# Weighted values over 64 keys a product, and an outer butterfly mixed while its matrix is turned

## The chip, the cores and the metric

The kernel runs on one core of a Trainium2 chip. A core has a matrix engine (TensorE, PE in the profile; PEld is its weight load), VectorE (DVE), ScalarE (ACT), GpSimd (POOL), a queue engine (SyncE, SP) and 16 DMA engines. The metric is the device time of one execution in microseconds (us); less is better. All data are float32.

## What is computed

Four layers in a row on x of 32 x 256 x 128, each `x = x + layer(layernorm(x))`: window attention, a butterfly FFN, linear attention, and the same FFN again. What matters here:

```python
# window attention: 16 heads of 8, 2 key heads, windows of 32 queries over 64 keys
scores = jnp.einsum('bhntd,bhnud->bhntu', qb, kb)
win_mask = (u >= t) & (u < t + W)            # t in 0..31, u in 0..63
probs = jax.nn.softmax(jnp.where(win_mask, scores, -jnp.inf), axis=-1)
out = jnp.einsum('bhntu,bhnud->bhntd', probs, vb)
# FFN: h = x @ W_exp + b_exp; nine butterfly stages; gelu; nine more; @ W_con
# stage s pairs feature i with i ^ 2**s:  na = w00 * a + w01 * b;  nb = w10 * a + w11 * b
```

Of every window's 64 keys exactly 32 count for each query: key u if u >= t in the first half, key u if u - 32 < t in the second.

## The kernel before, in words

The 8192 rows are cut into 16 groups of 512 rows (4 tiles of 128, two batches). A group passes through stages named P (input, keys and queries), W (window attention), F (first FFN), L (linear attention) and G (second FFN). Each engine's program is one list of steps, run in turns: `due(t, lag)` runs a step for group t - lag, so steps of up to eight groups are in flight. The tables PRODUCTS, VECTOR, PHI, PROBS and so on repeat that order, and the counts that one engine waits for on another are worked out from them. So the order on every engine is written out by hand, and each queue runs strictly in order. TensorE's results go to four ring banks in PSUM, one pair of banks for scores (`ps_s`) and one for weighted values (`ps_o`). On SP's queue stand the loads of x, the keys' and values' round trip through DRAM (`store_keys`, `spread_keys` with 8 DMAs, `spread_values` with 8 DMAs) and the stores of the result. `kx` has one buffer: the keys of a group are spread only when all four score products of the group ahead are done.

Window attention for one tile j (a chunk; four chunks a group, 64 in all):

- `scores` (L491): 8 products into `ps_s`; a row of `ps_s` is a query, 64 score columns for each of 16 heads.
- VectorE: `merge_halves` (L1018) puts the second half's score over the first's where t < row, so that 32 of 64 columns remain per head; `row_max` (L1025), `subtract_max` (L1031), and `scores_transposed` (L1038) in blocks of 32 by 32.
- ScalarE: `probs_out` (L810) writes exp of 512 values a row to `probs_m`.
- GpSimd: `probs_parted` (L419) writes `probs_t`, twice as wide: the same 512 values times either of two 0/1 masks `keep`, one part for each half of the keys.
- TensorE: `weighted_values` (L508): 16 products of 32 keys each; those of the second half add to the first's in PSUM. A row of ones in the values gives the sum of probabilities.
- VectorE: `head_outputs` (L1045 to L1052) transposes, takes the reciprocal and scales.

The FFN's nine butterfly stages are folded once, at the start, into one matrix each way. For the up matrix, seven inner stages go through TensorE (`up_stage`, L626, steps X.u0a to X.u6b) and ScalarE (L861); two outer stages, which pair whole blocks of 128 features, ran on VectorE (`up_outer_stage` by `outer_stage`, L286 and L289); `up_transposed` (L648) turns the four blocks with a matrix transpose against the identity, and ScalarE copies them to `w1b`. The down matrix has its outer stages first, on VectorE (`down_outer_stage`, `d_t`), then L640.

```python
nc.tensor.matmul(ps_o[32 * c:32 * c + 32, a, 0:HPK * WIN], vx[rows, j, a, u],
                 probs_t[rows, j % 2, u, a], start=(u == 0), stop=(u == PARTS - 1))
```

Of the kernel before, what the change touches and what calls it, by code (L numbers as in the profile page):

```python
# [9 lines left out]
ALU = mybir.AluOpType  # L10
# [7 lines left out]
WIN = 32  # L18
# [11 lines left out]
PARTS = SPAN // WIN  # L30
STAGES = HID.bit_length() - 1
INNER = P.bit_length() - 1
KVW = DIM + HEADS
FIRST = [("ident", P), ("last_half", WIN), ("keep", PARTS * WIN), ("wq", P), ("wkv", 2 * KV * HD), ("bq", 1), ("bkv", 1), ("inside", TSPAN), ("bo", P)]
# [33 lines left out]
]  # L68
PHI = [
    ("L.k1", 5), ("L.q", 4), ("L.k0", 4),  # L70
]
PROBS = [
    ("W.E3", 3), ("W.E0", 2), ("W.E1", 2), ("W.E2", 2),
# [1227 lines left out]
```

## Time and profile before

| | before |
|---|---|
| median of 3 runs | 597.85 us (596.56 to 598.96) |
| profiled execution, its own time | 597.42 us |
| its span | 595.6 us |
| TensorE busy, products | 553.9 us, 93% (6068) |
| TensorE weight loads | 355.3 us, 60% |
| VectorE | 445.7 us, 75% |
| ScalarE | 336.7 us, 57%, of it 77.0 for 60 table loads |
| GpSimd | 446.7 us, 75%, of it 150.4 for 64 masks |
| mean DMA rate | 38 GB/s |

The span is the time from the first to the last event of the profiled execution; its own time is what the same metric as the runs' gives for it. The share of busy time is an average over the filling, the middle and the end. Matmuls are counted by pass: each float32 product shows as two.

### The profile page before, as it was taken

What the parts mean: (1) busy time and instruction counts of PE and PEld (TensorE: products, weight loads), DVE (VectorE), ACT (ScalarE), POOL (GpSimd) and SP (SyncE); (2) the same over time, 40 slices, a digit from 0 to 9 for tenths busy, and PEclk for the clock granted to TensorE, in tenths of its full rate; (3) what the DMA queues carried; (4) which work ended last, traced back from release to release, by engine and by line L of the source; (5) the groups of instructions that cost most, each with busy time, mean ns of one, the idle gap of its engine ahead of it and who ended that gap; (6) DMA issues with size and microseconds to landing.
All of it is one profiled execution on the core that took longest, in us unless ns stands there. A gap on an engine that the chain in (4) does not pass through costs nothing.

```text
span 595.6 us, 16572 instructions
## 1 busy us (share of the span) xinstructions
PE 553.9 (93%) x6068; PEld 355.3 (60%) x6068; DVE 445.7 (75%) x1270; ACT 336.7 (57%) x574; POOL 446.7 (75%) x645
## 2 busy tenths in 40 slices
PE   3867698989999999999999999999999999999986
PEld 2533354556756656666666675665666666777663
DVE  5498878898888878787887888787877878654430
ACT  1321355366667666665666566766666666766532
POOL 6064778798979878897979798887887795956530
PEclk9996989999999999999999999999999999999998
DMA  9410201010101020111101010101010100000001
GB/s 316 134 37 15 52 7 46 13 41 16 39 24 46 25 47 20 33 37 29 43 21 43 16 42 26 45 26 43 21 34 20 29 24 2 19 3 19 0 19 35
DMA packets 37904, 22.48 MB, mean 38 GB/s; under 512 B 8384, under 2 KB 35520, under 8 KB 37824
## 3 DMA queue, kind: packets, MB, share of 16 engines
q1 hardware_dynamic: 35376, 17.21, 11.1%
q10 hardware_dynamic: 2448, 4.22, 2.0%
q8 instruction: 48, 0.79, 0.6%
q14 instruction: 32, 0.26, 0.2%
HBM read 15.91 MB, written 5.51 MB: 36 GB/s over the span
## 4 chain that ended last, share of the span: by engine, by line
PE 82%; DVE 7%; issue 3%; POOL 2%; DMA 1%; ACTq 1%; SPq 1%; ACT 1%; DVEq 0%; POOLq 0%
PE ring L523 20%; PE ring L535 18%; PE ps_o L508 10%; PE ps_s L491 9%; PE ring L472 7%; PE ring L546 5%; PE ring L566 4%; PE ring L606 3%; PE ring L555 2%; PE ring L583 2%; PE ring L576 1%; DVE u_t L289 1%; SPq L328 1%; DMA x_P<-in_x 1%; PE ring L595 1%
## 5 line engine op out<-in xcount | busy, mean ns | idle before, releaser
L419 POOL TENSOR_TENSOR probs_t<-probs_m,first 128x1024 f32<-128x1024 f32 x64 | 150.4, 2362 | 34.7 <-ACT probs_m L810 26.3
L792 ACT ACT_TABLE_LOAD x60 | 77.0, 1283 | 10.8 <-issue 9.7
L802 ACT ACTIVATE hid_G<-ring,b 128x512 f32<-128x512 f32 x64 | 44.0, 687 | 62.0 <-PE ring L523 61.2
L491 PE MATMUL ps_s<-kx,q_t 64*32 64x512 f32 x1024 | 71.0, 611 | 6.8 <-DVE merged L1031 4.3
L508 PE MATMUL ps_o<-probs_t,vx 32*32 32x256 f32 x2048 | 72.5, 392 | 3.1 <-DVE vx L1113 2.8
L523 PE MATMUL ring<-xT_G,w1b 128*128 128x512 f32 x128 | 65.7, 619 | 1.7 <-DVE x_F L1003 1.0
L1018 DVE COPY_PREDICATED ps_s<-first,ps_s 128x512 f32<-128x512 uint32 x64 | 43.6, 682 | 28.0 <-PE ps_s L491 27.6
L535 PEld LDWEIGHTS ring<-w,hid_G 128*128 128x128 f32 x512 | 59.5, 192 | 3.5 <-ACT hid_G L802 1.7
L535 PE MATMUL ring<-w,hid_G 128*128 128x128 f32 x512 | 59.9, 275 | 1.8 <-DVE x_L L1003 1.0
L523 PE MATMUL ring<-xT_F,w1b 128*128 128x512 f32 x128 | 59.2, 605 | 0.7 <-ACT xT_F L780 0.7
L535 PE MATMUL ring<-w,hid_F 128*128 128x128 f32 x512 | 59.9, 275 | 0.0
L535 PEld LDWEIGHTS ring<-w,hid_F 128*128 128x128 f32 x512 | 58.6, 192 | 0.8 <-issue 0.8
L802 ACT ACTIVATE hid_F<-ring,b 128x512 f32<-128x512 f32 x64 | 43.9, 687 | 23.3 <-PE ring L523 23.2
L810 ACT ACTIVATE probs_m<-merged_t 128x512 f32<-128x512 f32 x64 | 39.4, 620 | 22.4 <-POOL probs_t L419 17.2
L1045 DVE STREAM_TRANSPOSE ps_o<-ps_o 128x512 f32<-128x512 f32 x64 | 45.5, 711 | 7.6 <-PE ps_o L508 7.3
L508 PEld LDWEIGHTS ps_o<-probs_t,vx 32*32 32x32 f32 x2048 | 31.5, 106 | 29.1 <-DVE mv_W L982 10.6
L1031 DVE TENSOR_TENSOR merged<-ps_s,rowmax 128x512 f32<-128x512 f32 x64 | 44.0, 687 | 2.8
L523 PEld LDWEIGHTS ring<-xT_F,w1b 128*128 128x128 f32 x128 | 23.0, 189 | 36.4 <-issue 34.5
L1038 DVE STREAM_TRANSPOSE merged_t<-merged 128x512 f32<-128x512 f32 x64 | 44.4, 695 | 0.2 <-ACT probs_m L810 0.2
L1025 DVE TENSOR_REDUCE rowmax<-ps_s 128x16 f32<-128x512 f32 x64 | 43.1, 674 | 0.9 <-issue 0.3
L523 PEld LDWEIGHTS ring<-xT_G,w1b 128*128 128x128 f32 x128 | 21.4, 194 | 22.3 <-issue 21.3
L566 PEld LDWEIGHTS ring<-later,xT_L 128*128 128x128 f32 x128 | 23.2, 189 | 14.7 <-issue 12.3
(114 smaller groups left out, 1071.5 us busy)
## 6 DMA issues: line engine op xcount, KB each, us to landing
kx<-kv_rows SPq DMA_DIRECT2D x128, 40.0 KB, 2.2
x_P<-in_x SPq DMA_DIRECT2D x16, 256.0 KB, 3.2
out_x<-x_G SPq DMA_DIRECT2D x16, 256.0 KB, 2.3
vx_t<-kv_rows SPq DMA_DIRECT2D x128, 8.0 KB
up_s<-in_up_m ACTq DMA_DIRECT2D x7, 256.0 KB, 7.0
down_s<-in_down_m ACTq DMA_DIRECT2D x7, 256.0 KB, 6.9
kv_rows<-kv_t SPq DMA_DIRECT2D x16, 80.0 KB, 1.6
later<-in_later_c SPq DMA_DIRECT2D x1, 584.0 KB, 4.1
```

The source lines that it names most:

```text
L419: nc.gpsimd.tensor_tensor(probs_t[:, j % 2].rearrange("p u k h t -> p u (k h) t"), probs_m[:, j % 2].rearrange("p (a k) h t -> p a (k h) t ...
L491: last = nc.tensor.matmul(ps_s[32 * i:32 * i + 32, a], q_t[half, P * j + 32 * c:P * j + 32 * c + 32], kx[half, :, TSPAN * j + 32 * c:TSPAN ...
L508: last = nc.tensor.matmul(ps_o[32 * c:32 * c + 32, a, 0:HPK * WIN], vx[rows, j, a, u], probs_t[rows, j % 2, u, a], start=(u == 0), stop=(u ...
L523: nc.tensor.matmul(bank(name)[:], w1b[:, P * c:P * (c + 1)], x_t[s][:], start=True, stop=True).then_inc(product.sem, 1)
L535: last = nc.tensor.matmul(bank(name)[:, P * j:P * (j + 1)], hid[s][:, c, P * j:P * (j + 1)], w2[:, c], start=(c == 0), stop=(c == CH - 1))
L566: last = nc.tensor.matmul(bank(name)[:, 2 * P * i:2 * P * (i + 1)], x_t["L"][:, P * j:P * (j + 1)], wl_s[:, P:3 * P], start=True, stop=True)
L792: nc.scalar.activation(unused[:, i:i + 1], half[0:1, 0:1], function)
L802: nc.scalar.activation(hid[s][:, c], bank(name)[:], ACT.Gelu, bias=b1[:, c:c + 1]).then_inc(drained[BANK[name]].sem, 1)
L1018: nc.vector.copy_predicated(merged_s, last_half.bitcast(mybir.dt.uint32).rearrange("p (a t) -> p a t", a=1) .to_broadcast([P, HEADS, WIN]) ...
L1031: nc.vector.tensor_tensor(merged[:, j % 2].rearrange("p k h t -> p (k h) t"), halves()[0], m, ALU.subtract).then_inc(drained["S"].sem, 1)
L1038: nc.vector.transpose(merged_t[:, j % 2].rearrange("p k h t -> p (k h t)"), merged[:, j % 2].rearrange("p k h t -> p (k h t)")).then_inc(v ...
L1045: nc.vector.transpose(ps_o[:, :, 0:HPK * WIN], ps_o[:, :, 0:HPK * WIN]).then_inc(vec.sem, 1)
```

## The change

**Weighted values.** The value rows are laid out so that 64 rows of the array hold both halves of a window's 64 keys (WINDOW, `spread_values`); a chunk is then 8 products of 64 rows by 32 columns, each complete in itself. Its moving operand needs the probabilities of one window on both halves of the 64 rows. `probs_out` therefore writes exp of the scores twice (1024 values a row, straight to `probs_t`, which now has four buffers, one for each chunk), and the new `spread_probs` on SP's queue overwrites, with 4 DMAs a chunk of 32 rows x 2 KB each, one copy on every block of 32 rows by its neighbour's. `probs_parted` then masks in place, with a mask chosen by the row. `probs_m` is gone.

**Butterfly.** `up_outer_stage` is gone. `up_diagonals` on GpSimd multiplies the coefficients of both outer stages into 16 numbers a row (`up_mix`) and those with the identity into 16 diagonal blocks (`up_diag`). `up_transposed` multiplies each of the four blocks with a row of four diagonal blocks and adds up in PSUM, so mixing and turning are one product. `up_bias_out` mixes the bias column on VectorE.

**Order.** All orders are new (lags are counted from another start, which by itself moves nothing; TURNS goes from NG + 7 to NG + 10 for that). The table rows are left out of the diff, and the lists of `turn` too.

```diff
@@
-FIRST = [("ident", P), ("last_half", WIN), ("keep", PARTS * WIN), ("wq", P), ...
+FIRST = [("ident", P), ("last_half", WIN), ("keep", WIN), ("wq", P), ...
-WINDOW = [[0, 1, 2, 3], [1, 0, 3, 2]]
+WINDOW = [[0, 1, 2, 3], [2, 3, 0, 1]]
-        vx = sb("vx", [P, TILES, KV, PARTS, 32])
+        vx = sb("vx", [P, TILES, KV, PAIR, 32])
-        probs_m = sb("probs_m", [P, 2, KV, HPK, WIN])
-        probs_t = sb("probs_t", [P, 2, PARTS, KV, HPK, WIN])
+        probs_t = sb("probs_t", [P, TILES, PAIR, KV, HPK, WIN])
@@ spread_values
-                        c = WINDOW[kv][i]
+                        c = WINDOW[kv][i & ~1] + i % PARTS
+            def spread_probs(g, j):
+                sp.wait_ge(probs.sem, probs.after(g, f"W.E{j}"))
+                for i in range(4):
+                    own, other = slice(32 * i, 32 * i + 32), slice(32 * (i ^ 1), 32 * (i ^ 1) + 32)
+                    sp.dma_start(probs_t[other, j, i % PAIR].rearrange("p k h t -> p (k h t)"),
+                                 probs_t[own, j, i % PAIR].rearrange("p k h t -> p (k h t)")
+                                 ).then_inc(spread[j].sem, 16)
+            def up_diagonals():
+                pool.wait_ge(outer_in, 16)
+                pool.wait_ge(first_in, 16)
+                for far in range(2):
...
+                    nc.gpsimd.tensor_tensor(
+                        up_mix[:, 2 * far:2 * far + 2].rearrange("p f (b o) -> p f b o", b=2), near.to_broadcast([P, 2, 2, 2]),
+                        outer_far.to_broadcast([P, 2, 2, 2]), ALU.mult).then_inc(up_mixed, 1)
+                pool.wait_ge(up_mixed, 2)
+                for c in range(CH):
+                    nc.gpsimd.tensor_tensor(
+                        up_diag[:, c], ident.rearrange("p (a n) -> p a n", a=1).to_broadcast([P, CH, P]),
+                        up_mix[:, c].rearrange("p (o a) -> p o a", a=1).to_broadcast([P, CH, P]), ALU.mult
+                    ).then_inc(up_diag_made, 1)
@@ probs_parted
-                pool.wait_ge(product.sem, product.after(g if j >= 2 else g - 1, f"W.PV{(j - 2) % 4}"))
-                pool.wait_ge(probs.sem, probs.after(g, f"W.E{j}"))
+                pool.wait_ge(spread[j].sem, spread[j].after(g, f"W.d{j}"))
+                parts = probs_t[:, j].rearrange("p s k h t -> p (s k h) t")
                 nc.gpsimd.tensor_tensor(
-                    probs_t[:, j % 2].rearrange("p u k h t -> p u (k h) t"),
-                    probs_m[:, j % 2].rearrange("p (a k) h t -> p a (k h) t", a=1).to_broadcast([P, PARTS, HEADS, WIN]),
-                    keep.rearrange("p (u a t) -> p u a t", u=PARTS, a=1).to_broadcast([P, PARTS, HEADS, WIN]), ALU.mult
+                    parts, parts, keep.rearrange("p (a t) -> p a t", a=1).to_broadcast([P, PAIR * HEADS, WIN]), ALU.mult
                 ).then_inc(parted.sem, 1)
@@ weighted_values
-                for u in range(PARTS):
+                for s in range(PAIR):
                     for a in range(KV):
-                        for i in range(4):
-                            rows, c = slice(32 * i, 32 * i + 32), WINDOW[a][i]
-                            last = nc.tensor.matmul(ps_o[32 * c:32 * c + 32, a, 0:HPK * WIN], vx[rows, j, a, u],
-                                                    probs_t[rows, j % 2, u, a], start=(u == 0), stop=(u == PARTS - 1))
+                        for b in range(2):
+                            rows, c = slice(64 * b, 64 * b + 64), WINDOW[a][2 * b + s]
+                            last = nc.tensor.matmul(ps_o[32 * c:32 * c + 32, a, 0:HPK * WIN], vx[rows, j, a, s],
+                                                    probs_t[rows, j, s, a], start=True, stop=True)
@@ up_transposed
-                pe.wait_ge(up_outer, 4 * CH)
+                pe.wait_ge(up_diag_made, CH)
                 for c in range(CH):
-                    last = nc.tensor.transpose(bank("X.wT")[:, P * c:P * (c + 1)], u_t[INNER % 2][:, c, 0:P],
-                                               ident[:])
+                    last = nc.tensor.matmul(bank("X.wT")[:], u_t[INNER % 2][:, c, 0:P],
+                                            up_diag[:, c].rearrange("p o n -> p (o n)"), start=(c == 0), stop=(c == CH - 1))
@@ probs_out
-                act.wait_ge(parted.sem, parted.after(g if j >= 2 else g - 1, f"W.um{(j - 2) % 4}"))
+                act.wait_ge(product.sem, product.after(g - 1, f"W.PV{j}"))
                 act.wait_ge(vec.sem, vec.after(g, f"W.tr{j}"))
-                nc.scalar.activation(probs_m[:, j % 2].rearrange("p k h t -> p (k h t)"),
-                                     merged_t[:, j % 2].rearrange("p k h t -> p (k h t)"), ACT.Exp
-                                     ).then_inc(probs.sem, 1)
+                scores = merged_t[:, j % 2].rearrange("p (a k) h t -> p a (k h t)", a=1)
+                nc.scalar.activation(probs_t[:, j].rearrange("p s k h t -> p s (k h t)"),
+                                     scores.to_broadcast([P, PAIR, HEADS * WIN]), ACT.Exp).then_inc(probs.sem, 1)
@@ host
-    keep = np.concatenate([row >= t, row < t], axis=1).astype(np.float32)
+    keep = np.where(np.arange(P)[:, None] // WIN % PARTS == 0, row >= t, row < t).astype(np.float32)
```

Where instructions stand, at three places. (L508 becomes L548, L491 becomes L531; `ps_o` are weighted values, `ps_s` scores.) First TensorE in the middle of the program, around chunk 3 and chunk 0 of two groups. Before:

```order
L508 MATMUL ps_o<-probs_t,vx 32x256 x16
L491 MATMUL ps_s<-kx,q_t 32x512 x8
L523 MATMUL ring0<-xT_G,w1b 128x512
L606 MATMUL ring1<-kvs,phi_q 128x144 x2
L523 MATMUL ring3<-xT_G,w1b 128x512
L523 MATMUL ring2<-xT_G,w1b 128x512
L472 MATMUL ring0<-first,o_w 128x128 x4
L472 MATMUL ring3<-first,o_l 128x128 x4
L523 MATMUL ring1<-xT_G,w1b 128x512
L583 MATMUL ring2<-xT_P,first 128x512
```

Now:

```order
L575 MATMUL ring2<-w2,hid_F 128x128 x16
L512 MATMUL ring0<-first,xn_L 128x128 x4
L512 MATMUL ring3<-first,o_l 128x128 x4
L548 MATMUL ps_o<-probs_t,vx 32x256 x8
L531 MATMUL ps_s<-kx,q_t 32x512 x8
L563 MATMUL ring0<-xT_G,w1b 128x512
L623 MATMUL ring2<-xT_P,first 128x512
L563 MATMUL ring1<-xT_G,w1b 128x512
L512 MATMUL ring3<-first,o_w 128x128 x4
L512 MATMUL ring0<-first,xn_P 128x128 x4
```

Scores and weighted values still stand in pairs, and a pair's weighted values belong to the group ahead; the transposes of `xn_L` and `o_l` and the query product have moved around them.

Second SP's queue in one period in the middle. Before:

```order
L346 DMA out_x<-x_G 128x4x128
L319 DMA kv_rows<-kv_t 128x160
L328 DMA kx<-kv_rows 16x4x160 x8
L302 DMA x_P<-in_x 128x4x128
L340 DMA vx_t<-kv_rows 8x4x64 x8
```

Now:

```order
L355 DMA probs_t<-probs_t 32x512 x8
L347 DMA vx_t<-kv_rows 8x4x64 x8
L326 DMA kv_rows<-kv_t 128x160
L362 DMA out_x<-x_G 128x4x128
L355 DMA probs_t<-probs_t 32x512 x4
L335 DMA kx<-kv_rows 16x4x160 x8
L355 DMA probs_t<-probs_t 32x512 x4
L309 DMA x_P1<-in_x 128x4x128
```

Sixteen copies of probabilities are new; four of them (chunk 0) stand ahead of the keys, four (chunk 1) right behind, eight (chunks 2 and 3 of that group) ahead of the values.

Third ScalarE at the start, behind its 17 DMA issues. Before:

```order
L792 ACT_TABLE_LOAD
L792 ACTIVATE unused<-half 1x1
L774 ACTIVATE xT_P<-ring 128x2x256
L861 ACTIVATE u_t<-ring 128x258 x6
L844 ACTIVATE q_t<-ring,first 128x512
```

Now:

```order
L833 ACT_TABLE_LOAD
L833 ACTIVATE unused<-half 1x1
L902 ACTIVATE u_t<-ring 128x258 x4
L815 ACTIVATE xT_P<-ring 128x2x256
L902 ACTIVATE u_t<-ring 128x258 x3
```

Four copies of up stages (0a, 0b, 1a, 2a) now stand ahead of the transposed input of group 0. Likewise on VectorE the down outer stages now stand ahead of the first `kv_t`.

## Rows read from the trace of the kernel before

**Rows 1.** Busy time by engine (instructions), 250 to 370 us

```profile
250.00:370.00 120.00, 120.00 (x1403) 78.12 (x1402) 98.98 (x289) 78.02 (x132) 103.70 (x151) 1.00 0.13 33
```

**Rows 2.** Passes of the query product, 275 to 350 us: durations, first and last start

```profile
L583 PE MATMUL ring<-xT_P,first x6: 592/592/592, 280.2 to 345.5; 128*128 128x512 f32 x6
```

**Rows 3.** TensorE in order of time, 337 to 352 us: start, us, what

```profile
338.16 1.09 PE L508 MATMUL ps_o<-probs_t,vx 32*32 32x256 f32 x32
339.19 1.09 PE L491 MATMUL ps_s<-kx,q_t 64*32 64x512 f32 x16
340.20 1.13 PE L523 MATMUL ring<-xT_G,w1b 128*128 128x512 f32 x2
...
341.66 1.88 PE L523 MATMUL ring<-xT_G,w1b 128*128 128x512 f32 x4
343.37 0.60 PE L472 MATMUL ring<-first,o_w 128*128 128x128 f32 x4
...
350.60 1.09 PE L491 MATMUL ps_s<-kx,q_t 64*32 64x512 f32 x16
```

**Rows 4.** Groups of instructions by shape: busy, mean ns, idle before

```profile
L419 POOL TENSOR_TENSOR probs_t<-probs_m,first 128x1024 f32<-128x1024 f32 x64 | 150.4, 2362 | 34.7 <-ACT probs_m L810 26.3 <-PE ps_s L491 8.4
...
L406 POOL TENSOR_TENSOR xb_L<-x_L,bffn_s 128x512 f32<-128x512 f32 x16 | 20.4, 1276 | 1.1 <-DVE x_G L1003 1.1
...
L818 ACT ACTIVATE phi_k<-neg_k 128x256 f32<-128x256 f32 x32 | 13.4, 418 | 1.0
...
L818 ACT ACTIVATE phi_q<-neg_q 128x512 f32<-128x512 f32 x16 | 10.1, 631 | 0.5
```

**Rows 5.** GpSimd in order of time, 325 to 358 us, idle before in brackets

```profile
333.80 4.68 POOL L419 TENSOR_TENSOR probs_t<-probs_m,first 128x1024 f32<-128x1024 f32 x2 [0.69 <-PE ps_s L491]
340.54 0.24 POOL L378 TENSOR_SCALAR rv_F<-mv_F 128x4 f32<-128x4 f32 x1 [2.05 <-DVE mv_F L982]
...
349.33 0.24 POOL L378 TENSOR_SCALAR rv_W<-mv_W 128x4 f32<-128x4 f32 x1 [0.31 <-DVE mv_W L982]
```

**Rows 6.** SP's queue in order of time, 310 to 358 us

```profile
340.43 5.01 SPq L328 DMA_DIRECT2D kx<-kv_rows  x8
...
349.58 3.52 SPq L340 DMA_DIRECT2D vx_t<-kv_rows  x8
```

**Rows 7.** The keys' DMAs: time of an issue, and from issue to landing

```profile
L328 SPq DMA_DIRECT2D kx<-kv_rows x128: 532/595/1605, 17.5 to 474.7; - x128
...
DMA to landing us min/median/max: 2.1/2.2/3.2
```

**Rows 8.** TensorE in order of time, 0 to 75 us

```profile
24.83 1.09 PE L491 MATMUL ps_s<-kx,q_t 64*32 64x512 f32 x16
...
36.05 1.09 PE L491 MATMUL ps_s<-kx,q_t 64*32 64x512 f32 x16 [0.62 <-DVE merged L1031]
...
47.74 1.96 PE L491 MATMUL ps_s<-kx,q_t 64*32 64x512 f32 x16 [1.47 <-DVE merged L1031]
...
63.69 1.09 PE L491 MATMUL ps_s<-kx,q_t 64*32 64x512 f32 x16 [0.97 <-DVE merged L1031]
...
71.60 1.09 PE L491 MATMUL ps_s<-kx,q_t 64*32 64x512 f32 x16 [2.43 <-issue]
```

**Rows 9.** VectorE in order of time, 0 to 75 us

```profile
12.71 0.38 DVE L968 SCALAR_TENSOR_TENSOR kv_t<-ring,first 128x160 f32<-128x160 f32 x1 [3.02 <-PE ring L576]
...
36.86 6.18 DVE L289 SCALAR_TENSOR_TENSOR u_t<-u_t,outer,u_tmp 128x129 f32<-128x129 f32 x4
...
45.65 1.14 DVE L289 SCALAR_TENSOR_TENSOR u_t<-u_t,outer,u_tmp 128x129 f32<-128x129 f32 x4
```

**Rows 10.** ScalarE in order of time, 9 to 25 us

```profile
11.15 0.57 ACT L774 ACTIVATE xT_P<-ring 128x512 f32<-128x512 f32 x1
13.73 0.66 ACT L861 ACTIVATE u_t<-ring 128x258 f32<-128x258 f32 x2 [2.01 <-PE ring L626]
15.45 0.39 ACT L861 ACTIVATE u_t<-ring 128x258 f32<-128x258 f32 x1 [1.06 <-PE ring L626]
```

More of the change, by code:

```diff
@@ L262, in window_and_linear_attention_with_butterfly_ffn @@
         kx_in = Count(sem("kx_in"), [("P.kx", 0)], 16 * HPK)
+        spread = [Count(sem(f"spread{j}"), [(f"W.d{j}", 0)], 16 * 4) for j in range(TILES)]
         v_in = Count(sem("v_in"), [("P.v", 0)], 16 * 4 * KV)
@@ L442, in turn @@
                 for g in due(t, 2):
-                    probs_parted(g, 1)
-                for g in due(t, 6):
-                    add_bias(g, "L", bffn_s, "L.proj", "G.down")
+                    probs_parted(g, 0)
                 for g in due(t, 1):
@@ L449, in turn @@
                     normalise(g, "W")
-                for g in due(t, 4):
-                    add_bias(g, "F", bproj_s, "F.down", "L.proj")
+                for g in due(t, 2):
+                    probs_parted(g, 1)
+                for g in due(t, 3):
+                    add_bias(g, "W", bffn_s, "W.proj", "F.down")
             for t in range(TURNS):
@@ L657, in turn @@
+                for g in due(t, 6):
+                    ffn_up(g, "F", 1)
+                    ffn_up(g, "F", 3)
+                    ffn_up(g, "F", 0)
+                    ffn_up(g, "F", 2)
+                for g in due(t, 7):
+                    linear_out(g, 1)
+                for g in due(t, 4):
+                    scores(g, 2)
                 for g in due(t, 5):
-                    linear_out(g, 1)
+                    weighted_values(g, 2)
+                for g in due(t, 7):
+                    linear_out(g, 0)
@@ new lines, in turn @@
+                if t == 5:
+                    up_stage(6, "b")
+                for g in due(t, 5):
+                    weighted_values(g, 3)
+                for g in due(t, 4):
+                    scores(g, 3)
+                for g in due(t, 8):
+                    ffn_up(g, "G", 0)
+                if t == 3:
+                    up_stage(3, "a")
+                for g in due(t, 3):
+                    attention_q(g)
+                for g in due(t, 8):
+                    ffn_up(g, "G", 2)
@@ new lines, in turn @@
+                if t == 4:
+                    up_stage(5, "a")
+                for g in due(t, 5):
+                    project(g, "W", o_wt, wo_s)
+                if t == 5:
+                    up_transposed()
+                for g in due(t, 6):
+                    norm_transposed(g, "L", "F")
+                for g in due(t, 8):
+                    ffn_up(g, "G", 1)
+                for g in due(t, 2):
+                    attention_kv(g)
+                if t == 3:
+                    up_stage(4, "a")
@@ new lines, in turn @@
+                if t == 7:
+                    up_weights_out()
+                for g in due(t, 8):
+                    linear_k_parts(g, 1)
+                if t == 1:
+                    up_stage_out(1, "a")
+                if t == 5:
+                    up_stage_out(4, "b")
+                for g in due(t, 8):
+                    linear_k_parts(g, 0)
+                if t == 5:
+                    down_stage_out(1)
+                if t == 2:
+                    up_stage_out(2, "a")
@@ new lines, in turn @@
+                if t == 7:
+                    down_stage_out(6)
+                for g in due(t, 8):
+                    linear_q_parts(g)
+                for g in due(t, 7):
+                    copy_out(g, "F.xT", x_t["F"][:], *UPS["F"])
+                if t == 5:
+                    down_stage_out(2)
+                if t == 6:
+                    up_stage_out(5, "a")
+                if t == 4:
+                    up_stage_out(1, "b")
+                for g in due(t, 6):
+                    probs_out(g, 3)
@@ new lines, in turn @@
+                for g in due(t, 7):
+                    gelu(g, "F", 1)
+                if t == 4:
+                    up_stage_out(2, "b")
+                if t == 6:
+                    down_stage_out(4)
+                    up_stage_out(6, "a")
+                    down_stage_out(5)
+                if t == 0:
+                    up_stage_out(0, "a")
+                if t == 5:
+                    up_stage_out(4, "a")
+                for g in due(t, 7):
+                    gelu(g, "F", 3)
@@ L953, in _ @@
+                for g in due(t, 7):
+                    copy_out(g, "L.xT", x_t["L"][:], "L.q", "L.k0", "L.k1")
             load_butterflies()
```

444 lines of the change are left out of this document (196 added, 248 removed), and 56 rows, old and new, of tables (COVERED, PRODUCTS, VECTOR).

## The prediction

> **What bounds the kernel now.** I read the page first (its numbers stand in the table above), then the busy times of a stretch in the middle, single engines' rows in order of time there, then the same for the first 80 us. Between 250 and 370 us TensorE is busy for all 120 us, while VectorE has 99.0, ScalarE 78.0 and GpSimd 103.7 us of work [rows 1]. So in the middle every microsecond taken from TensorE counts until the next engine is full, and idle time of the others costs nothing. One group of 512 rows takes one period: the second pass of the query product recurs after three executions from 280.2 (first pass) to 345.5 us; less 0.4 for the pass, that is two periods of 32.45 us [rows 2].
>
> How much room have the others? GpSimd idles 0.69, 2.05 and 0.31 us in one period [rows 5], so its floor is 32.45 - 3.05 = 29.4 us. VectorE's work is 99.0 / 120 of 32.45 = 26.8 us; dependent operations add short gaps, so I put its floor at 28. ScalarE's work is 21.1.
>
> The filling is different. Scores of group 0 start at 24.8 us, of group 1 at 47.7, of group 2 at 71.6; the last of group 1's four score products is at 63.7 [rows 8]. TensorE has gaps there, and VectorE and the keys are what it waits for.
>
> **The change part by part.**
>
> *Weighted values.* Before, 16 products per chunk, 32 rows by 32 columns of the array, two for each of eight places, 256 columns wide. Each product is two passes. A chunk takes from 338.16 to 339.19, 1.03 us. A pass of 512 columns takes 0.43 us (four from 341.66 to 343.37), one of 256 therefore 0.213 [rows 3]. Four rounds of eight such passes are 0.85; the remaining 0.17 is start-up. After, 8 products of 64 rows by 32 columns stand on eight different places: two rounds, 0.43 + 0.17 = 0.60 us. The score products have that shape today, also 8, 64 by 32, but 512 columns wide: 339.19 to 340.20, 1.01 us = 0.85 + 0.16 [rows 3]. So a chunk gives 0.42 us and 64 chunks 27. Only those that run while TensorE is full shorten the path: groups 2 to 15, 56 chunks, 23.6 us. The first eight lie in the filling, costed apart. The new period is 32.45 - 4 x 0.42 = 30.8.
>
> No row tells what the 0.17 us is. The Trainium skill, TensorEngine Tiling (Array Packing), Key Properties, says that a change of tiling mode drains TensorE. By that rule scores and weighted values, now of one shape and next to each other, would drain once instead of twice; a rival below does the like.
>
> *Exponentials.* ScalarE writes 1024 values a row instead of 512. From 0.418 us at 256 to 0.631 at 512 [rows 4] 256 cost 0.21, so 0.43 more for each, 1.7 us a period: 22.8 of 30.8 us, hidden. Without that cover it would be 27 us in all.
>
> *Copies of probabilities.* Four DMAs per chunk on SP's queue, 16 a period. SP now issues in a period 8 for the keys in 5.01 us, 8 for the values in 3.52 [rows 6] and three single ones, which at 0.44 (3.52 / 8) make 9.8 us together. At 0.44 to 0.63 (5.01 / 8) 16 more cost 7 to 10; I take 8.5. SP then issues for 18 of 30.8 us. A landing takes 2.2 us [rows 7]. Exponential, four issues, landing and mask become 1.06 + 2.1 + 2.2 + 2.4 = 7.8 us where it was 3.0 [rows 4]. That stays hidden: a chunk's weighted values stand a whole period behind its scores in both orders. Queued behind these copies on SP are the keys of the next group: those of chunk 0 stand ahead of them. Chunk 0's scores are 8 us ahead of the end of a period, and ScalarE reaches that exponential once the GELUs of the F stage are done, some 6 us before the last scores of the group, which the keys wait for anyway. The keys need 5.0 us of issues and 2.2 of landing, 7.2 [rows 6, 7]; between the last scores of a group and the first of the next TensorE had 350.60 - 340.20 = 10.4 us of other work [rows 3], and has 8.3 now (the products between them in the new order, by their rows). Slack falls from 3.2 to 1.1 us.
>
> *Mask on GpSimd.* Same count, 1024 values, 2.36 us each [rows 4], now in place. I take the same. Two 512-wide additions would be 2 x 1.27 = 2.54 [rows 4], which adds 0.7 us a period, to 30.1, still under 30.8; a gain as large is the lower bound. Along the new order GpSimd waits some 1.3 us a period for moments of the F stage, and its results reach TensorE 1 to 3 us early at five hand-overs. For margins that fail I add 1 us in all, between 0 and 14 x 0.5.
>
> *Outer butterfly.* Out go the up stages on VectorE: 6.18 and 1.14 us of multiply-adds [rows 9] and the multiplications ahead of each, some 9 us between the scores of group 0 and 1. Without them group 1's first scores are bound by the keys. The new transposing product has eight passes of 512 columns, 3.4 us, where four transposes take 0.6 [rows 3]: 2.8 more on TensorE, in a stretch where it idles for longer; I take 1, bounds 0 and 2.8. GpSimd gets four products of 512 values, 4 x 1.27 = 5.1 us [rows 4], before it normalises group 1, which is not needed for 9 us more. VectorE runs the down stages at that time. The 6.18 us ran beside GpSimd's masks, the 1.14 did not, for equal work [rows 9]: that prices such a meeting.
> The Trainium skill, SBUF — State Buffer, SBUF: two separate sides, has the rule: a VectorE operation with two SBUF inputs and a GpSimd one that reads SBUF exclude each other. By it the new diagonals can hold up the eight down multiply-adds, just ahead of the first keys. The trace agrees (6.18 against 1.14).
>
> *The start.* Before, ScalarE first drains the transposed input, at 11.15 us [rows 10], and all up to the scores at 24.8 hangs on that. Now four copies of butterfly stages stand ahead, two of them one after another through TensorE at 1.7 us a stage (13.73 to 15.45, [rows 10]), the last copy 0.39: 3.8 us later. VectorE drains the keys at 12.71 [rows 9], now due at 16.5; with down stages ahead that meet the diagonals (up to 5 us, 6.18 less 1.14) it is free between 13 and 18. The delay is 3.8 to 5.5; I take 3.9. First scores at 28.7; the fourth 11.2 later as before (24.8 to 36.0, [rows 8]), 39.9; then keys, 1.1 + 7.2 and 0.8 for hand-overs, group 1 at 49.0; the copies of chunk 1 stand behind those keys and those of 2 and 3 behind them, so masks of group 0 end near 58.7; behind its weighted values the last scores of group 1 at 59.3 instead of 63.7; 9.1 later as above, group 2 at 68.4. That is 3.2 us ahead of 71.6.
>
> **Sum.** Profiled execution 597.42 us (span 595.6), median of the runs 597.85: 0.4 apart, which I leave. 597.4 - 23.6 - 3.2 + 1 (transposing product) + 1 (margins) = 572.6. Its own range is 566 to 579.
>
> **The rivals.**
> *GpSimd sets the pace.* For: its floor of 29.4 is 95% of 30.8, and landings and moments now wait in one queue. Against: it idles 3 us a period today. With masks 0.4 us longer and 0.6 us of waits left the period is 29.4 + 1.6 + 0.6 = 31.6: 14 x 0.85 = 12, the start 3.2: 582.
> *One start-up less.* Where the two kinds of 64 by 32 products follow each other, up to 0.17 us of start-up goes too: 56 x 0.17 = 9.5, so 562. For: nothing in the rows binds the 0.17 to a shape. Against: GpSimd's floor is then 0.7 us from the period.
> *No overlap.* If the 64-row products ran four at a time, a chunk would stay at 1.03 and only start and transposing product would count: 597.4 - 3.2 + 1 = 595.2. The score rows speak against it.
> *SP's queue is full: slower.* At (32.45 - 9.8) / 16 = 1.42 us an issue the queue takes as long as a period of before, keys come late, and each period grows. One issue of keys did take 1.6 us [rows 7]; at that the period is 9.8 + 25.6 = 35.4, 14 x 2.9 = 41 more: 637. Against: the median issue is 0.6.
>
> **How the numbers follow.** Forecast 0.61, GpSimd's pace 0.18, one start-up less 0.10, no overlap 0.04, SP 0.07. Within 0.5% (about what a measurement of this kernel can tell) is 594.9 to 600.8: the no-overlap case and a thin edge, 0.05. Slower 0.06, faster 0.89. The range is 561 to 587: it takes in one start-up less and GpSimd's pace with margin, and leaves out the two others.
>
> **What would show it.** Right: a chunk of weighted values holds TensorE for 0.60 us; the period is 30.8 with TensorE still full; first scores near 28.7, group 2's near 68.4; SP issues for under 20 us a period. Wrong: TensorE waits for masks or keys in every period; GpSimd has no idle time; a chunk takes 1 us; first scores after 31.

## The result, and the profile after

The changed kernel takes **568.64 us** (median of four runs, 566.75 to 569.98), the kernel before 597.2 on the same chip (596.21 to 598.96): a ratio of 0.952, 95% interval 0.9499 to 0.9542. Forecast were 572.6 us, between 561 and 587. The profiled execution took 568.07 us (span 566.3). It is compared with 597.42 of before: 29.3 us less, where the sum had 24.8.

The page of the changed kernel: busy time by engine, the granted clock in 40 slices, four of its groups, and one line of DMA issues:

```profile
PE 521.8 (92%) x5048; PEld 344.3 (61%) x5048; DVE 436.6 (77%) x1256; ACT 352.2 (62%) x570; POOL 451.9 (80%) x651
...
PEclk9969999998999999999999999999999999999999
...
L459 POOL TENSOR_TENSOR probs_t<-probs_t,first 128x1024 f32<-128x1024 f32 x64 | 151.5, 2368 | 10.8 <-DMA probs_t<-probs_t 10.8
L852 ACT ACTIVATE probs_t<-merged_t 128x1024 f32<-128x1024 f32 x64 | 67.1, 1048 | 54.2 <-DVE merged_t L1090 46.2
...
L531 PE MATMUL ps_s<-kx,q_t 64*32 64x512 f32 x1024 | 71.5, 615 | 8.0 <-DVE merged L1083 5.3
...
L548 PE MATMUL ps_o<-probs_t,vx 64*32 64x256 f32 x1024 | 42.3, 387 | 3.7 <-POOL probs_t L459 2.0
...
probs_t<-probs_t SPq DMA_DIRECT2D x256, 64.0 KB, 2.0
```

A mask costs what it did (2.368 us against 2.362, [rows 4]). The exponential takes 1.048 us, as worked out. The 256 copies land 2.0 us after their issue. GpSimd waited for them 10.8 us in all, in four waits, all in the filling.

The same stretch as in [rows 1], busy time of each engine, then granted clock, DMA share and GB/s:

```profile
core 0: us, PE busy (x) PEld busy (x) DVE busy (x) ACT busy (x) POOL busy (x), PEclk, DMA share, GB/s
250.00:370.00 120.00, 119.44 (x1220) 79.54 (x1220) 103.04 (x306) 87.18 (x140) 109.71 (x160) 1.00 0.28 70
```

TensorE is still the full engine. GpSimd's share of the stretch rose from 103.7 to 109.7 us with the same work in shorter periods.

TensorE's timeline of the changed kernel, in order of time (start and duration in us, engine, line, what, tiles of the array, operand, number of passes; in brackets how long the engine was idle before and for whom). Each piece is a pair of scores (L531) and weighted values (L548), with the product ahead of it and, in the first and last piece, the one behind it:

```profile
302.61 0.48 PE L616 MATMUL ring<-xT_P,first 128*32 128x160 f32 x8
303.02 0.66 PE L548 MATMUL ps_o<-probs_t,vx 64*32 64x256 f32 x16
303.47 1.06 PE L531 MATMUL ps_s<-kx,q_t 64*32 64x512 f32 x16
304.47 0.48 PE L606 MATMUL ring<-later,xT_L 128*128 128x256 f32 x1
...
323.27 0.60 PE L512 MATMUL ring<-first,o_l 128*128 128x128 f32 x4
323.80 0.66 PE L548 MATMUL ps_o<-probs_t,vx 64*32 64x256 f32 x16
324.26 1.06 PE L531 MATMUL ps_s<-kx,q_t 64*32 64x512 f32 x16
...
341.74 0.46 PE L635 MATMUL ring<-v_ext,phi_k 128*32 128x33 f32 x32
342.13 1.09 PE L531 MATMUL ps_s<-kx,q_t 64*32 64x512 f32 x16
343.01 0.64 PE L548 MATMUL ps_o<-probs_t,vx 64*32 64x256 f32 x16
343.58 1.98 PE L563 MATMUL ring<-xT_F,w1b 128*128 128x512 f32 x4
```

Read the distances between starts, since the ends are modelled. From 342.13 to 343.58 a pair takes 1.45 us; from 303.02 to 304.47 also 1.45. Before it took 2.04 (338.16 to 340.20, [rows 3]). So a chunk gives 0.59 us, not 0.42: from the first to the second of a pair there is only its work (0.45 us from 303.02 to 303.47, 0.88 from 342.13 to 343.01), and the start-up shows once, at the end of the pair.

From the same timeline the scores of the filling, as in [rows 8], the turning product, and the query product twice, one period apart, as in [rows 2]:

```profile
27.76 1.09 PE L531 MATMUL ps_s<-kx,q_t 64*32 64x512 f32 x16
...
48.28 1.09 PE L531 MATMUL ps_s<-kx,q_t 64*32 64x512 f32 x16 [2.25 <-DMA kx<-kv_rows]
...
61.32 1.09 PE L531 MATMUL ps_s<-kx,q_t 64*32 64x512 f32 x16 [0.63 <-DVE merged L1083]
...
65.80 3.60 PE L690 MATMUL ring<-up_diag,u_t 128*128 128x512 f32 x8
...
70.86 1.09 PE L531 MATMUL ps_s<-kx,q_t 64*32 64x512 f32 x16 [0.45 <-DMA kx<-kv_rows]
...
152.25 1.06 PE L531 MATMUL ps_s<-kx,q_t 64*32 64x512 f32 x16
...
174.99 1.02 PE L623 MATMUL ring<-xT_P,first 128*128 128x512 f32 x2
...
205.22 1.02 PE L623 MATMUL ring<-xT_P,first 128*128 128x512 f32 x2
```

A period is 205.22 - 174.99 = 30.23 us; before it was 32.45. Three of the ten behind group 5 are 0.2 to 0.5 us longer, so the mean is 30.33. Where the 29.3 us came from, cut at two query products that both kernels have: the one of group 5 starts 5.6 us earlier (144.76 against 150.37), the ten periods from there to group 15's last 303.25 us against 324.56 and give 21.3, and what comes behind it 2.4. In another execution of the changed kernel (e11 below) the cuts fall at 6.7, 20.7 and 2.5.

### The profile page after: what moved, and what is told of

The parts are those of the page before. It is cut to its first block, busy times and chain, and to the rows that moved or that the text cites. A ratio compares the mean times of both kernels' runs of the same rounds, so it can differ in the third digit from the quotient of the medians.

```text
span 566.3 us, 14624 instructions
## 1 busy us (share of the span) xinstructions
PE 521.8 (92%) x5048; PEld 344.3 (61%) x5048; DVE 436.6 (77%) x1256; ACT 352.2 (62%) x570; POOL 451.9 (80%) x651
## 4 chain that ended last, share of the span: by engine, by line
PE 79%; DVE 8%; POOL 5%; issue 3%; ACT 2%; ACTq 2%; SPq 1%; DMA 0%; DVEq 0%; POOLq 0%
PE ring L563 20%; PE ring L575 18%; PE ps_s L531 9%; PE ring L512 6%; PE ring L586 5%; PE ps_o L548 4%; PE ring L606 4%; PE ring L646 3%; PE ring L623 2%; POOL probs_t L459 2%; PE ring L595 2%; PE ring L666 1%; DVE merged L1083 1%; PE ring L616 1%; DVE ps_s L1070 1%
## 5 line engine op out<-in xcount | busy, mean ns | idle before, releaser
L459 POOL TENSOR_TENSOR probs_t<-probs_t,first 128x1024 f32<-128x1024 f32 x64 | 151.5, 2368 | 10.8 <-DMA probs_t<-probs_t 10.8
L852 ACT ACTIVATE probs_t<-merged_t 128x1024 f32<-128x1024 f32 x64 | 67.1, 1048 | 54.2 <-DVE merged_t L1090 46.2
L531 PE MATMUL ps_s<-kx,q_t 64*32 64x512 f32 x1024 | 71.5, 615 | 8.0 <-DVE merged L1083 5.3
L548 PE MATMUL ps_o<-probs_t,vx 64*32 64x256 f32 x1024 | 42.3, 387 | 3.7 <-POOL probs_t L459 2.0
L563 PEld LDWEIGHTS ring<-xT_F,w1b 128*128 128x128 f32 x128 | 23.3, 192 | 30.3 <-issue 29.4
L563 PEld LDWEIGHTS ring<-xT_G,w1b 128*128 128x128 f32 x128 | 20.7, 190 | 22.5 <-ACT xT_G L821 12.4
L548 PEld LDWEIGHTS ps_o<-probs_t,vx 64*32 64x32 f32 x1024 | 15.2, 106 | 30.0 <-issue 21.8
```

The lines of the kernel that those rows point to most:

```text
L459: nc.gpsimd.tensor_tensor(parts, parts, keep.rearrange("p (a t) -> p a t", a=1).to_broadcast([P, PAIR * HEADS, WIN]), ALU.mult).then_inc(p ...
L531: last = nc.tensor.matmul(ps_s[32 * i:32 * i + 32, a], q_t[half, P * j + 32 * c:P * j + 32 * c + 32], kx[half, :, TSPAN * j + 32 * c:TSPAN ...
L548: last = nc.tensor.matmul(ps_o[32 * c:32 * c + 32, a, 0:HPK * WIN], vx[rows, j, a, s], probs_t[rows, j, s, a], start=True, stop=True)
L563: nc.tensor.matmul(bank(name)[:], w1b[:, P * c:P * (c + 1)], x_t[s][:], start=True, stop=True).then_inc(product.sem, 1)
L852: nc.scalar.activation(probs_t[:, j].rearrange("p s k h t -> p s (k h t)"), scores.to_broadcast([P, PAIR, HEADS * WIN]), ACT.Exp).then_inc ...
```

## The experiments

"Over e11" means over 568.43 us, the changed kernel measured once more. Of the runs only e9 and e10 share a chip with e11. All were measured against the kernel before on their own chip, whose median was between 597.0 and 597.35 each time.

### The two parts apart (e1, e2)

e1 is the kernel before with this in it:

```diff
+                if t == 1:
+                    up_diagonals()
...
-                    last = nc.tensor.transpose(bank("X.wT")[:, P * c:P * (c + 1)], u_t[INNER % 2][:, c, 0:P],
-                                               ident[:])
+                    last = nc.tensor.matmul(bank("X.wT")[:], u_t[INNER % 2][:, c, 0:P],
+                                            up_diag[:, c].rearrange("p o n -> p (o n)"), start=(c == 0), stop=(c == CH - 1))
...
-                if t == 2:
-                    up_outer_stage(0)
...
-                    up_outer_stage(1)
+                    up_bias_out()
```

> The kernel before with the butterfly part of the change alone (diagonals on GpSimd, turning and mixing in one group of products on TensorE, the bias column in three small VectorE steps). Theory A (the two parts add up; the filling gained because VectorE lost some 9 us of outer stages): group 1's first scores a little ahead of the 47.7 us of before, group 2's 1 to 3 us ahead of 71.6, period unchanged at 32.45, time 594 to 596.5 us. Rival B (the diagonals and the four 512-column products cost what VectorE gives back): 597 to 599 us. Rival C (most of the 29 us gained come from here): below 585.

Measured: 594.50 us (593.92 to 595.79), ratio 0.996, interval 0.9946 to 0.9974. That is the time of theory A. Group 1's first scores came at 43.9 us, group 2's at 67.1, 3.9 and 4.5 ahead of before: more than I expected. 1.0 us of it stands already at group 0's first scores (23.83 against 24.83), where TensorE left a slow stretch sooner in this execution (last section); it is not the butterfly's. 1.3 is gone by group 5 (152.7 against 155.9). The period stayed 32.45.

e2 is the changed kernel with the opposite edit; both outer stages stand in one go where the changed kernel mixes the bias, not apart as in the kernel before.

> The changed kernel with the outer stages of the up butterfly put back on VectorE and four plain transposes on TensorE: the weighted values' part and the new order alone. Theory A (filling bound by VectorE without the other part): period 30.2 us as in the changed kernel, group 2's first scores 3 to 6 us after the 70.9 of the changed kernel, time 571 to 575 us. Rival B (masks and keys, not VectorE, bound the filling): 568 to 570 us, no difference.

Measured: 571.13 us (569.38 to 574.16), ratio 0.9571 (0.9529 to 0.9613, which just overlaps that of the change). Period 30.2. Group 2's first scores are only 0.8 us later than in the changed kernel (71.67), but this execution was 1.6 us ahead at group 0's (26.13 against 27.76). Group 2's third chunk is 4.2 later (85.34 against 81.17) and group 5's first 3.1 (155.37 against 152.25). TensorE's timeline of e2:

```profile
68.85 1.11 PE L664 MATMUL ring<-first,u_t 128*128 128x128 f32 x4 [4.66 <-DVE u_t L291]
...
80.54 4.87 PE L539 MATMUL ring<-xT_F,w1b 128*128 128x512 f32 x8
```

TensorE waits 4.66 us for the outer stages on VectorE. Its granted clock falls within that wait and reads 0.50 from 66 to 72 us and again from 76 to 82, so the first products of the F stage take 4.80 us to the next scores, where the changed kernel takes 3.64 at a clock of 1.00 (77.53 to 81.17). So the time is theory A's, the place a little behind the one named, and part of the 4.2 us is TensorE's clock and not VectorE's work. The parts add up: e1 gave 2.9 us, e2 26.2, together 29.1; the changed kernel has 28.6 to 28.8.

### What a round costs (e3)

```diff
-                for s in range(PAIR):
+                for s in [0, 1, 0, 1]:
```

> The changed kernel with each weighted-value product issued twice (the second overwrites the first with the same values): 16 instead of 8 products of 64 by 32 in a chunk. Theory A (a chunk is rounds of 0.213 us with one start-up shared with the scores): 0.43 us more a chunk, period 30.2 + 1.7 = 31.9, time 568.6 + 24 to 26 = 593 to 595 us. Rival B (each round costs a start-up of its own, 0.17): 0.77 more a chunk, period 33.3, about 612 us. Rival C (TensorE is no longer the engine that sets the pace): under 15 us more.

Measured: 591.61 us (588.96 to 593.21), 23.2 over e11. TensorE's timeline of e3, the same place as 323.80 above:

```profile
338.15 1.09 PE L548 MATMUL ps_o<-probs_t,vx 64*32 64x256 f32 x32
339.03 1.06 PE L531 MATMUL ps_s<-kx,q_t 64*32 64x512 f32 x16
```

0.88 us where it was 0.46, so two more rounds of passes cost 0.42, and no start-up goes with a round. Nor is it the mere number of passes that sets this time: at 341.74 above 32 passes of 33 columns take 0.39 us, less than the 0.42 of these 16. The period is 31.96 (query products at 181.19 and 213.15), 1.73 more: 4 times 0.43. Theory A for the middle; the total is 1.4 us under its span, which may be the filling, where a chunk need not cost its full time; that was not looked into. It also says that TensorE's time counts one to one from 30.2 us upwards.

### Is a start-up saved by standing side by side? (e5, e6)

Moving steps changes which waits others cover. So e5 empties that list, and e6 is e5 with the weighted values moved:

```diff
-COVERED = {
...
+COVERED = set()
```

> The changed kernel with no wait left out: the list of waits that others cover is emptied, so each is issued. It is the control for the two kernels below. Theory A: a wait that is already met costs TensorE nothing that is seen, 568 to 569.5 us. Rival B: each costs some tens of ns on TensorE's sequencer, 570 to 574 us.

Measured: 571.24 us (569.0 to 571.54), ratio 0.9564 (0.9537 to 0.9591), 2.8 over e11. That speaks for rival B, not strongly: the interval just overlaps that of the change (up to 0.9542), though not that of e11 (up to 0.9527). The middle holds under 1 us of it (nine periods from 174.80 to 448.41, 30.40 each, against 30.34 for the changed kernel between 174.99 and 448.01). The rest is not in the trace: the execution profiled was the fastest of the four, 569.0 us, the others 571.1 to 571.5.

```diff
-                for g in due(t, 5):
-                    weighted_values(g, 1)
...
+                for g in due(t, 5):
+                    weighted_values(g, 1)
+                for g in due(t, 6):
```

(Chunk 1 now stands behind the first product of the F stage. Likewise chunk 2 stands behind a product of the L stage, chunk 3 ahead of the transposes of `o_l`, and chunk 0 ahead of the keys' product.)

> The kernel of e5 with the four chunks of weighted values moved in the order so that none stands next to scores; each now follows and precedes other products. Theory A (adjacent products of one shape save a start-up of about 0.16 us per pair): 4 x 0.16 = 0.64 us a period more, 15 groups, e5 + 9 to 10 us, and a chunk of weighted values takes 0.60 us. Rival B (0.60 was wrong for another reason, the shape itself has less start-up): e5 + 0 to 2 us.

Measured: 585.99 us (584.67 to 590.79), **14.8 over e5**. TensorE's timeline of e6; the order is that of 323.27 above, but with the weighted values one step earlier:

```profile
334.17 0.60 PE L496 MATMUL ring<-first,xn_L 128*128 128x128 f32 x4
334.70 0.66 PE L532 MATMUL ps_o<-probs_t,vx 64*32 64x256 f32 x16
335.29 0.65 PE L496 MATMUL ring<-first,o_l 128*128 128x128 f32 x4
335.88 1.09 PE L515 MATMUL ps_s<-kx,q_t 64*32 64x512 f32 x16
336.90 1.12 PE L547 MATMUL ring<-xT_G,w1b 128*128 128x512 f32 x2
...
344.49 0.66 PE L532 MATMUL ps_o<-probs_t,vx 64*32 64x256 f32 x16
345.08 0.48 PE L600 MATMUL ring<-xT_P,first 128*32 128x160 f32 x8
345.49 1.09 PE L515 MATMUL ps_s<-kx,q_t 64*32 64x512 f32 x16
```

Standing alone, the weighted values take 0.59 us (the 0.60 of the prediction), and the four transposes behind them also 0.59, where such four take 0.44 side by side with their like (322.83 to 323.27 in the changed kernel: 0.44). Each change of shape costs its own start-up, on the way in and on the way out. Apart, a chunk and its scores have four such changes, side by side two. Chunk 0 is the exception: the keys' product that parts it (345.08) has tiles of 128 by 32 and stood ahead of the pair as a change already, so there only one is new. That makes seven more changes a period. The period is 31.44 (nine from 180.76 to 463.76) against 30.40, 1.04 more, 0.15 a change. Periods in which TensorE waits for nothing last 31.42 (212.18 to 243.60) and 30.28 (235.44 to 265.72 in e5): 1.14 more, 0.16 a change. Compared between the same products in both kernels, chunk 0 pays 0.11 us for its one change, and chunks 1, 2 and 3 pay 0.36, 0.25 and 0.42 for two each. So theory A's 0.16 was right, and its 9 to 10 us too small by a third because I had counted four changes a period. Against before the count is three (in, from values to scores of another shape, out) and now two; that is the one start-up less. The runs show what a change costs, not what the engine does in that time.

### How far GpSimd is (e4, e7)

e4 gives GpSimd one more addition of 512 values in each group:

```diff
+                    nc.gpsimd.tensor_tensor(extra[:], up_diag[:, 0], up_diag[:, 1], ALU.add).then_inc(extra_made, 1)
```

> The changed kernel with one more addition of 512 values on GpSimd in every group (16 in all, 1.0 to 1.3 us each), at the end of its turn. GpSimd idles 0.9 us in a period now. Theory A (GpSimd is hidden but close): 0 to 0.3 us a period, 568.6 to 573 us, and GpSimd's idle time nearly gone. Rival B (GpSimd already sets the pace): the full 1.0 to 1.3 us a period, 583 to 589 us. Rival C (ample room): no difference.

Measured: 573.52 us (569.26 to 574.96), 5.1 over e11: just beyond theory A, far below B. GpSimd's timeline of e4, where it waits for no other engine between 223 and 254 us, and TensorE's timeline there:

```profile
252.49 1.31 POOL L495 TENSOR_TENSOR extra<-up_diag 128x512 f32<-128x512 f32 x1
253.73 2.38 POOL L461 TENSOR_TENSOR probs_t<-probs_t,first 128x1024 f32<-128x1024 f32 x1
```

```profile
213.46 0.67 PE L552 MATMUL ps_o<-probs_t,vx 64*32 64x256 f32 x16 [0.38 <-POOL probs_t L461]
```

That wait, 0.4 us for the mask, recurs at 244.23, 274.91 and 305.60, and the period is 30.7. Take off the added 1.24 us (252.49 to 253.73), and GpSimd's own floor is 29.4 to 29.5, where the prediction had 29.4. TensorE at 30.23 stands 0.8 above it.

e7 takes the mask out (the `probs_t` product of GpSimd becomes `pass`, and TensorE waits for the copies instead).

> The changed kernel without the mask: GpSimd multiplies nothing, and the probabilities are not masked, so the kernel computes attention without its causal mask and window. GpSimd loses 9.5 us of work a period, the masks also leave its port and the chain. Theory A (GpSimd is hidden in the middle; only the filling waits for masks): period 30.2 unchanged, the filling 1 to 4 us shorter, 564 to 568 us. Rival B (GpSimd sets the pace, or its masks slow VectorE on the path): period under 30.0, below 563 us.

Measured: 564.92 us (562.03 to 565.19). Theory A: the period is unchanged (nine, from 172.30 to 445.27, make 272.97 us; in the changed kernel, from 174.99 to 448.01, 273.02). The medians are 3.5 us apart from e11. Between the traces of e7 and the changed kernel 2.7 us are gone by group 5's first scores (149.56 against 152.25), and the query product of group 15 is no further ahead (445.27 against 448.01). Masks cost only in the filling.

### The copies (e9)

```diff
             def spread_probs(g, j):
+                if g > 0:
+                    return
...
-                pool.wait_ge(spread[j].sem, spread[j].after(g, f"W.d{j}"))
+                if g == 0:
+                    pool.wait_ge(spread[j].sem, spread[j].after(0, f"W.d{j}"))
+                else:
+                    pool.wait_ge(probs.sem, probs.after(g, f"W.E{j}"))
```

> The changed kernel with the copies of probabilities issued for group 0 alone; the masks of later groups wait for the exponential only. It leaves out the repeating of probabilities for groups 1 to 15, so half of each weighted sum uses stale values. SP's queue loses 240 of its 256 copies. Theory A (copies and their 2 us landings are hidden in the middle, and cost only where masks wait for them in the filling): period 30.2 unchanged, the filling 0.5 to 2.5 us shorter, 566 to 568.5 us. Rival B (keys or masks are late behind the copies in every period): period under 30.0, below 564 us. Rival C (nothing): 568.6 us.

Measured: 565.86 us (565.38 to 566.68), 2.6 under e11 on the same chip. Period unchanged (nine from 173.06 to 446.06, 30.33). The 16 copies a group and their landing are hidden in the middle and cost 1.5 us up to group 5 (query product at 142.15 against 143.65 in e11); the profiled executions as wholes are 1.5 apart too (566.03 and 567.54, the latter the fastest of its four), so the rest of the 2.6 does not show in the traces. The time lies 0.1 us under theory A's span, and the rest is as theory A says.

### The start (e8, e10, e11, e12)

e8 is e5 with group 0's keys ahead of the butterfly's first products, on all engines:

```diff
-                if t == 0:
-                    up_stage(0, "a")
...
-                if t == 1:
-                    down_outer_stage(1)
...
-                if t == 0:
+                if t == 1:
+                    attention_kv_out(0)
                     down_outer_stage(0)
+                    down_outer_stage(1)
```

> The kernel of e5 with the start in the order of before: group 0's transpose and keys ahead of the butterfly's first products and of the down outer stage. Theory A (the 3 us by which the first scores came later pass on to the end): first scores at 24.8 instead of 27.8 us, time e5 - 2.5 to e5 - 3.5 us. Rival B (group 2 is bound by the keys on SP's queue and by masks, whatever the start): first scores at 24.8, but group 2's as before, e5 within 1 us. Rival C (the butterfly comes later and with it the second matrix): e5 + 1 to + 4 us.

Measured: 569.59 us (566.45 to 571.01), 1.65 under e5; the ranges overlap. First scores came at 26.86, not 24.8: the keys were early, but I had left the query product behind more butterfly stages than before has there (22.54 against 20.28; in both executions products ran slowly until some 20 us, see below). None of the three theories fits as written.

e10 puts the list of covered waits of the changed kernel back into e8; e11 is the changed kernel on the same chip; e12 repeats e10.

> The changed kernel with the start of e8 (group 0's keys ahead of the butterfly's first products) and the same waits left out as in the changed kernel. Theory A (the start's gain is mostly lost by group 5, where GpSimd is the busy engine; what is left is what e8 had over e5): 0.5 to 1.7 us below e11. Rival B: no difference from e11 within 0.3 us.

> The changed kernel itself once more, as the control of e10 on the same chip: 568.6 us, 566.8 to 570.

> The kernel of e10 once more. In e10 TensorE reached its full rate at 14.5 us (eight butterfly products in 1.13 us), in e8, with the same order, only after 20 us (2.06 us for eight at 14.5). Theory A (the order itself is worth 3 us): 564.5 to 566.8 us again, first scores near 23.9. Theory B (most of the 3.1 us of e10 is the moment at which TensorE comes to full rate, which differs from run to run): 566.5 to 568.5 us, first scores near 26.5.

Measured: e10 565.29 us (564.48 to 566.78; ratio 0.9461, 0.9441 to 0.9481), e11 568.43 (567.54 to 569.17; 0.951, 0.9493 to 0.9527), e12 566.30 (564.51 to 566.71; 0.9486, 0.9464 to 0.9507). Both are under e11, by 3.1 and 2.1 us, and this start is the best version of the study. For e10 that is more than either theory allowed (at most 1.7). The intervals of e10 and e11 don't overlap, those of e12 and e11 do. TensorE's timeline of e10 and then of e12, one program:

```profile
14.45 1.13 PE L666 MATMUL ring<-u_t,up_s 128*128 128x129 f32 x8 [0.57 <-ACT u_t L899]
16.15 0.68 PE L666 MATMUL ring<-u_t,up_s 128*128 128x129 f32 x4 [0.57 <-ACT u_t L899]
17.40 0.68 PE L666 MATMUL ring<-u_t,up_s 128*128 128x129 f32 x4 [0.57 <-ACT u_t L899]
...
23.91 1.09 PE L531 MATMUL ps_s<-kx,q_t 64*32 64x512 f32 x16
```

```profile
14.57 2.06 PE L666 MATMUL ring<-u_t,up_s 128*128 128x129 f32 x8 [0.57 <-ACT u_t L899]
17.20 1.20 PE L666 MATMUL ring<-u_t,up_s 128*128 128x129 f32 x4 [0.57 <-ACT u_t L899]
18.97 1.20 PE L666 MATMUL ring<-u_t,up_s 128*128 128x129 f32 x4 [0.57 <-ACT u_t L899]
...
26.81 1.09 PE L531 MATMUL ps_s<-kx,q_t 64*32 64x512 f32 x16
```

The same eight products take 1.13 us in one execution and 2.06 in the other, and the first scores differ by 2.9 us. In the profiled executions of e5, e8 and e11 they are slow up to some 20 us as well. So theory B of e12 holds for the place of e10's first scores. The total doesn't decide: 566.30 lies inside theory A's span and 0.2 under theory B's. What the start is worth by itself is read from executions that are slow equally long: e12 stands 1.6 us ahead of e11 at the query product of group 15 (446.00 against 447.56), e8 0.7 ahead of e5 (447.74 against 448.41). e10 is 1.5 us further ahead at that place (444.46), with the program of e12. So the order is worth 0.7 to 1.6 us in the traces, half or less of the 3.1 between the medians of e10 and e11. In the traces the other 1.5 goes with the slow stretch. How long the executions without a trace were slow is not known.

## Why the prediction was right, point by point

The measured 568.64 us lie between the forecast of 572.6 and the rival "one start-up less", put at 562 (572.6 less its 9.5 makes 563.1). The forecast is the nearer of the two in time, but the trace shows the rival's chunk. The forecast's size of a chunk was wrong, the time came out inside its range all the same, and neighbours, longer periods and the end took back part of what the larger gain brought.

**The bound.** Right: TensorE is full in the middle before and after; e3 shows that its time counts one to one, e7 and e9 that masks and copies cost nothing there.

**Weighted values, 0.42 us a chunk.** Mechanism right, size short. The two rounds of 0.43 are there (e3), and alone a chunk takes 0.59 (e6). The step that failed is the count of start-ups: "the remaining 0.17 is start-up. After, ... 0.43 + 0.17 = 0.60". Beside scores of the same shape the 0.17 is paid once for both, and a pair gives 0.59. That was the rival with 0.10. It had deserved more than a tenth, since the row of scores and the row of values each had such a rest and the new order kept all four pairs side by side. The rule that the prediction cites (the Trainium skill, TensorEngine Tiling (Array Packing), Key Properties: a change of tiling mode drains TensorE) fits what the runs show, about 0.16 us for a change (e6).

**The period, 30.8.** Measured 30.23. Ten periods gave 21.3 us, where the sum had 40 chunks of 0.42, 16.8, less the 0.7 of margins that were not the filling's: 5.2 us more. Taken with 0.3 more in the filling and 1.0 less in the tail, that is the difference of 4.5 between forecast and result. At 0.59 the 40 chunks make 23.6, so 2.3 did not arrive: 0.13 us in each period went to neighbours of the pairs in the new order (4 x 0.59 = 2.36 against 32.46 - 30.23 = 2.23, between 247.74 and 280.20 before), and 0.9 in all to the longer periods.

**GpSimd.** Its floor of 29.4 was right (e4), and the mask's unchanged 2.36. "GpSimd sets the pace" did not come; it is 0.8 us away.

**Copies.** Issues took 0.59 us (median; 0.44 to 0.63 taken), landing 2.0 (2.2 taken). With 9.7 us for the others in SP's timeline of one period, SP issues for 16 x 0.59 + 9.7 = 19.1 us; forecast 18. Hidden, with 1.5 to 2.6 us in the filling that the sum had in another term.

**Exponentials.** 1.05 us, hidden: ScalarE is at 87 of 120 us.

**The filling.** Up to group 5's query product 5.6 us were gained. The sum has there -3.2, +1 for the turning product, 0.3 for margins and 8 chunks of 0.42: -5.3. The total is right, the places are not, and it moves by 1.1 us from one execution to another (6.7 in e11). First scores 27.8 (28.7 forecast; the copy of the transposed input at 15.01, 3.9 later, as worked out, but the query product only 3.2). Group 1 at 48.3 (49.0), it waited 2.25 for keys as forecast. Its last scores at 61.3, 2.0 later than the 59.3 forecast, behind VectorE; group 2 at 70.9 (68.4). The 3.2 us said to be won by group 2 were 0.7 then, and came by group 5 with the chunks' share.

**Butterfly part.** The turning product took 3.60 us (3.4 forecast), and the part as a whole is worth 2.9 us alone (e1, where the start may have a share) and 2.5 in the changed order (e2, whose range overlaps).

**The tail.** 2.4 us, where eight chunks of 0.42 made 3.4 and eight of 0.59 would make 4.7. Why it gave half of that was not looked into.

**Waits on TensorE.** Margins were given 1 us; in the middle TensorE waits for no mask or key; the longer periods lose their time ahead of a product of the G stage, where it waits 0.18 and 0.38 us for ScalarE's transposed input (325.50 and 356.18).

## What to carry to other kernels

Count changes of shape on TensorE as an item of its own: each change cost about 0.16 us here, and products of one tiling side by side share them. When products get another tiling, ask first which neighbours have it, and then the cost of the products themselves. Test how far the next engine is by giving it one small operation more: it told GpSimd's floor to a tenth of a microsecond. Before two traces are compared in the filling, see whether TensorE ran at the same rate in both.

## What the runs showed of the hardware that was not expected

**A scalar multiply beside GpSimd.** VectorE's and GpSimd's timelines of the changed kernel, at the start:

```profile
9.13 3.27 DVE L293 TENSOR_SCALAR d_tmp<-d_t,outer 128x128 f32<-128x128 f32 x4
12.43 1.14 DVE L296 SCALAR_TENSOR_TENSOR d_t<-d_t,outer,d_tmp 128x128 f32<-128x128 f32 x4
13.61 0.88 DVE L293 TENSOR_SCALAR d_tmp<-d_t,outer 128x128 f32<-128x128 f32 x4
```

```profile
8.09 4.03 POOL L448 TENSOR_TENSOR up_diag<-first,up_mix 128x512 f32<-128x512 f32 x4
```

The prediction let the multiply-adds with two inputs meet the diagonals. It was the four multiplications, with one input in SBUF, that took 3.27 us instead of 0.88, one for each diagonal; the multiply-adds, 1.14, came after. The Trainium skill has this too (SBUF — State Buffer, Who interferes with whom: `tensor_scalar` can enter a mode that holds the ports shared with GpSimd). The trace agrees: the four multiplications behind the diagonals take 0.88 us. It cost nothing here, since VectorE then waited 0.92 us for the keys' product.

**TensorE at half rate.** Three stretches of the changed kernel's filling, columns as in [rows 1]:

```profile
29.00:33.00 4.00, 2.03 (x24) 0.93 (x23) 3.16 (x5) 1.65 (x3) 0.00 (x0) 1.00 0.16 42
33.00:37.00 4.00, 2.03 (x17) 0.36 (x17) 2.87 (x11) 0.28 (x1) 0.65 (x3) 0.55 0.28 68
37.00:41.00 4.00, 3.49 (x24) 1.87 (x24) 3.29 (x5) 1.49 (x2) 3.74 (x8) 0.50 0.00 0
```

TensorE was busy for 2.03 of the 4 us from 29 to 33. The granted clock fell between 33 and 34, in a gap of 2.5 us ahead of the scores at 34.97, and stayed at 0.50, the lower of the two levels, until past 43. Every kernel here has such stretches in its filling, and they fall in different places: before from 43 to 53 and from 74 to 77, e1 from 23 to 27 and from 67 to 74. So places in the filling of two kernels differ by this as well as by the edit.

At the very start the rows of e10 and e12 differ by the same factor, 1.13 against 2.06, while the granted clock reads 1.00 in both. Why one execution of a program leaves that slow stretch before 14.5 us and another after 20 stays open. It moves the first scores by 2.9 us and the query product of group 15 by 1.5, as much as most of what was tested in the filling.
